# A depthwise wavelet convolution: from five tiles in two column phases to four in two and one in four

## The chip, the cores and the metric

The kernel runs on one core of a Trainium2 chip. The metric is the device time of one execution in microseconds; a kernel's time is the median of its runs. One further execution is taken by the hardware profiler, and all rows come from that one. TensorE (PE in rows; PEld is its weight load), VectorE (DVE), ScalarE (ACT), GpSimd (POOL) and SyncE (SP) each run their own instruction queue and synchronise by semaphores.

## What is computed

Two layers on an image batch `x` of shape (8, 96, 256, 256) in 32-bit floats. The first is a windowed linear attention and is not touched. The second adds to its input `x1`, after a group normalisation, a 5x5 depthwise convolution and a three-level Haar wavelet branch with its own 5x5 depthwise convolutions:

```python
for i in range(3):
    co = haar2d(cur)                 # four half-size images: sums and differences
    cur = co[:, :, 0]                # their low-pass one goes on to the next level
    flat = dwconv(co.reshape(B, C * 4, h, w), wconv_w[i]) * wscale[i]
    level_coeffs.append(flat.reshape(B, C, 4, h, w))
next_ll = zeros
for i in reversed(range(3)):
    next_ll = ihaar2d(level_coeffs[i] with next_ll added to its low-pass image)
out = x1 + dwconv(gn(x1), base_w) * base_scale + base_b + next_ll
```

The kernel folds level 1 of the wavelet and the base convolution into one linear map on the normalised image, so that only levels 2 and 3 are separate.

## The kernel before

The first stage computes the attention layer into `y_scratch` in device memory. The second stage, where the change lies, goes through the 96 channels, each in two groups of four images (192 groups). An image of 256 rows is cut into `WINDOWS = 5` tiles of 64 rows, of which 52 are kept (`OROWS`) and 4 on either side are halo. A tile stands on the partitions twice: 64 rows with the even columns and 64 rows with the odd ones (two column phases), 128 columns per image, 512 for four images. The convolution is then, per tile, five matrices of 128x128 (one per horizontal tap offset `d`), each applied to the tile shifted by `d`. Each 32-bit product is made as three matmuls of rounded parts: `split` issues high x high, high x low, low x high (L1312 to L1314). The results of the five tiles stay in five PSUM banks `ps_w`.

What each engine does for one group, in the order of its queue:

- SyncE (L1138 on): `group` waits until `make_x1` has freed the one pair of input buffers `xb`, `yb`, loads the rows of the group three ahead (10 DMAs), then `store` sends out the five output windows as they become ready. After the second group of a channel it loads the parameters and, once `mat23_ready` says that the last ones are used up, the raw matrices of the next channel with `load_raw` (10 DMAs).
- TensorE (`steps`, L1324): convolution of tiles 0 and 1; level 3 (20 matmuls, L1351 to L1354); level 2 (30 matmuls with 256 columns); tiles 2 to 4; the upsampling of `next_a` and `next_b` into all tiles (L1364, L1366); then `sum_down` (L1320) of the next group, which makes the low-pass image `ps_ll` for levels 2 and 3. `conv(t)` waits for `out_ready`, which says that VectorE has emptied the PSUM bank.
- VectorE (`steps`, L1465): `finish` of window 0 of the group before (bias and `x1` added, two column phases, L1458); `make_in`; `finish` of window 1; `split_in`; `finish` of windows 2 to 4; `make_x1` of the group two ahead (L1389); `trailing` of the next group, the low parts of its tiles (L1402, L1405); `up_levels`; `split_next`, which makes `next_lo`.
- ScalarE (`steps`, L1280): copies and high parts of levels 2 and 3; `norm` of the next group (16 operations, L1263); `leading`, its high parts (L1276 with a mask of zeros for rows beyond the image, L1278); the copy of level 3; the high parts of `next_ll` (L1297, L1298).
- GpSimd (L1216 on): `build` turns raw matrices into high and low parts: the convolution's once per channel, when `raw_in` says that they have landed (L1205, L1213), those of levels 2 and 3 when level 2 of the channel's second group is done (`l2_ready`).

At the start of the stage GpSimd sets whole buffers to zero (L1095) before SyncE issues the first raw load.

Of the kernel before, what the change touches and what calls it, by code (L numbers as in the profile page):

```python
# [21 lines left out]
F32 = mybir.dt.float32  # L22
F32R = mybir.dt.float32r
ALU = mybir.AluOpType
# [19 lines left out]
TAPS = 5  # L44
HALF = W // 2
WROWS = 64
# [9 lines left out]
NV1 = 4 * TAPS * 2  # L56
# [7 lines left out]
CHUNKS = PIECE // 512  # L64

# [8 lines left out]
def wt_attention_kernel(nc, x, wqkv_t, wp_t, gamma, beta, base_w, base_b, base_scale, wconv, wscale,  # L74
# [10 lines left out]
    with ExitStack() as ctx:  # L85
# [128 lines left out]
        with ExitStack() as ph:  # L214
# [62 lines left out]
            def _(pool):  # L277
# [30 lines left out]
                p1 = pad1.rearrange("p (ia q dj o n) -> p ia q dj o n", ia=2, q=2, dj=TAPS, o=2)  # L308
                for ia in range(2):
                    for q in range(2):  # L310
                        for oa in range(2):
                            for p in range(2):
                                o = 1 - p
                                first = WROWS - 3 - oa
                                full = p1[:, ia, q, :, o, first:first + 2 * TAPS - 1:2]
# [5 lines left out]
                                for n, dj in enumerate(djs):  # L321
                                    lo = first + 2 * dis[0]
                                    part = p1[:, ia, q, dj, o, lo:lo + 2 * len(dis) - 1:2]
# [692 lines left out]
        with ExitStack() as ph:  # L1016
# [14 lines left out]
            x1 = [sb_(f"x1_{s}", [128, PAIRW, IMGS, W]) for s in range(SLOTS)]  # L1031
# [3 lines left out]
            zb = [[sbr_(f"zb{g}_{h}", [128, WINDOWS, IMGS, ZW]) for h in range(2)] for g in range(SETS)]  # L1035
            raw1 = sb_("raw1", [128, 2 * TAPS, WROWS])
            raw2 = sb_("raw2", [128, 2 * TAPS, HALF])
            raw3 = sb_("raw3", [128, 2 * TAPS, HALF])
            mat1 = [[sbr_(f"mat1_{k}_{h}", [128, TAPS, 2 * WROWS]) for h in range(2)] for k in range(2)]
            mat2 = [sbr_(f"mat2_{h}", [128, 2, TAPS, HALF]) for h in range(2)]  # L1040
# [3 lines left out]
            down_sb = sbr_("down_sb", [128, WINDOWS, HALF])  # L1044
            UPPER = -(-(HALF // 2) // (OROWS // 2))
            LOWER = WINDOWS - HALF // OROWS
            up_sb = sbr_("up_sb", [128, UPPER + LOWER, 2 * WROWS])
            inside_sb = sb_("inside_sb", [128, PAIRW])
            mask = sb_("mask", [128, 2])
            zero1 = sb_("zero1", [128, 1])  # L1050
            z = sb_("z", [128, WINDOWS, IMGS, HALF])
# [21 lines left out]
            const_in, zeroed = sem_("constc_in"), sem_("zeroed")  # L1073
            xy_in, down_set, mask_set = sem_("xy_in"), sem_("down_set"), sem_("mask_set")
# [14 lines left out]
            NRAW = (4 + 2 + 4) * 16  # L1089
            GROUPS_C = C * SETS  # L1090

            def zero_pads(eng):

                for t_ in (xb, yb, *zb[0], *zb[1], *in2_p, in3_hl):
                    eng.memset(t_[:].bitcast(F32), 0.0).then_inc(zeroed, 1)  # L1095
                eng.memset(zero1[:], 0.0).then_inc(zeroed, 1)
# [6 lines left out]
            def slot(k, g):  # L1103
                return 2 * k + g
# [452 lines left out]
```

## Time and profile before

| | us |
|---|---|
| median of 3 runs | 10908.44 |
| lowest and highest run | 10892.28, 10910.33 |
| profiled execution | 10874.65 |
| its span | 10872.8 |
| second stage, from about | 5386 |
| TensorE busy over the span | 10462.5 (96%) |
| VectorE, ScalarE, GpSimd busy | 9149.1, 7181.6, 3711.4 |

The span is the time from the first instruction to the last; the profiled execution's own time is 1.85 us longer. Busy times are of one engine each and overlap between engines.

### The profile page before, as it was taken

To read this page: it belongs to the slowest core of one execution; us is meant where nothing else is said; L and a number is where in the kernel's file an instruction comes from. 1 tells how busy PE (TensorE), PEld (TensorE's weight loads), DVE (VectorE), ACT (ScalarE), POOL (GpSimd) and SP (SyncE) were. 2 spreads that over 40 slices of the span, in tenths; PEclk is the share of its full clock that TensorE was granted. 3 is DMA by queue.
4 is the path that set the end of the run, shared out by engine and by line. 5 is a ranking of instruction groups with operands and counts; after the bars stand their busy time and mean duration, and the time that the engine had idled before them with its cause. 6 is when DMAs were issued, how large, how long until landed. Compare 5 with 4: busy or idle time off the path is not lost.

```text
span 10872.8 us, 205183 instructions
## 1 busy us (share of the span) xinstructions
PE 10462.5 (96%) x66084; PEld 8922.4 (82%) x66084; DVE 9149.1 (84%) x16540; ACT 7181.6 (66%) x11852; POOL 3711.4 (34%) x3719
## 2 busy tenths in 40 slices
PE   4999999999999999999799999999999999999999
PEld 4888888888888888888678888888888888888887
DVE  6999999899999989988777777777777777777777
ACT  4887878778787777788555555555555555555554
POOL 3444444444444444444322222222222222222222
PEclk9999999999999999999899999999999999999999
DMA  5433333333433324322277777777777777777775
GB/s 188 136 95 127 113 113 132 106 119 102 136 113 109 130 92 136 112 72 81 71 155 153 157 157 154 155 153 154 158 155 155 154 153 155 158 154 156 154 152 125
DMA packets 1162869, 1453.49 MB, mean 134 GB/s; under 512 B 215391, under 2 KB 1125023, under 8 KB 1125279
## 3 DMA queue, kind: packets, MB, share of 16 engines
q1 hardware_dynamic: 1161055, 1442.80, 52.6%
q10 hardware_dynamic: 1376, 6.13, 0.1%
q8 instruction: 119, 1.95, 0.1%
q14 instruction: 319, 2.61, 0.1%
HBM read 1040.11 MB, written 408.56 MB: 133 GB/s over the span
## 4 chain that ended last, share of the span: by engine, by line
PE 28%; DVE 17%; issue 4%; ACT 1%; DMA 0%; SPq 0%; POOL 0%; DVEq 0%; POOLq 0%
PE ps_w L1312 5%; PE ps_w L1313 5%; PE ps_w L1314 5%; PE ps_ll L1320 4%; DVE ob L1458 4%; DVE x L1389 3%; DVE zb L1402 2%; DVE zb L1405 1%; PE ps_w L1364 1%; PE ps L1352 1%; PE ps_w L1366 1%; DVE sum L1429 1%; PE ps L1312 1%; PE ps L1313 1%; PE ps L1314 1%
## 5 line engine op out<-in xcount | busy, mean ns | idle before, releaser
L1312 PE MATMUL ps_w<-zb,mat 128*128 128x512 f32 x4800 | 1925.6, 401 | 8.8
L1313 PE MATMUL ps_w<-zb,mat 128*128 128x512 f32 x4800 | 1906.2, 397 | 0.0
L1314 PE MATMUL ps_w<-zb,mat 128*128 128x512 f32 x4800 | 1905.2, 397 | 0.0
L1458 DVE SCALAR_TENSOR_TENSOR ob<-ps_w,prm,x 64x512 f32<-64x512 f32 x1920 | 1440.7, 750 | 516.0 <-PE ps_w L1364 477.2
L641 POOL CAST xn_hi<-xs 96x512 fp32r<-96x512 f32 x1024 | 878.3, 858 | 2918.0 <-PE ps_qkv L666 2087.0
L1263 ACT ACTIVATE z<-x,prm 64x384 f32<-64x384 f32 (+1 forms) x3072 | 1813.7, 662 | 58.7 <-DVE x L1389 51.0
L1205 POOL CAST mat<-raw 128x1280 fp32r<-128x1280 f32 (+1 forms) x288 | 469.5, 1648 | 3942.6 <-DMA raw<-vec 2350.0
L664 PE MATMUL ps_qkv<-wqkv_hi,xn_hi 96*128 96x288 f32 x4096 | 1387.2, 339 | 47.1 <-issue 22.3
L643 POOL TENSOR_TENSOR xn_lo<-xs,xn_hi 96x512 fp32r<-96x512 f32 x1024 | 1355.8, 1324 | 81.9
L666 PE MATMUL ps_qkv<-wqkv_hi,xn_lo 96*128 96x288 f32 x4096 | 1212.1, 296 | 0.0
L665 PE MATMUL ps_qkv<-wqkv_lo,xn_hi 96*128 96x288 f32 x4096 | 1209.9, 295 | 0.0
L591 ACT ACTIVATE tok<-ps_qkv 128x1152 f32<-128x1152 f32 x1024 | 1160.4, 1133 | 0.0
L1312 PEld LDWEIGHTS ps_w<-zb,mat 128*128 128x128 f32 x4800 | 903.1, 188 | 303.1 <-DVE ob L1458 91.2
L1314 PEld LDWEIGHTS ps_w<-zb,mat 128*128 128x128 f32 x4800 | 901.9, 188 | 226.8
L1313 PEld LDWEIGHTS ps_w<-zb,mat 128*128 128x128 f32 x4800 | 901.6, 188 | 209.6
L686 PE MATMUL ps_num<-kv_sb,q_sb 104*128 104x104 f32 x8192 | 1070.2, 274 | 0.0
L702 PE MATMUL ps_f<-att,wp_sb 96*96 96x512 f32 x2048 | 1052.9, 595 | 8.2 <-DVE f_cur_b L176 3.1
L686 PEld LDWEIGHTS ps_num<-kv_sb,q_sb 104*128 104x128 f32 x8192 | 1026.4, 193 | 0.1
L1283 ACT ACTIVATE ll<-ps_ll 128x512 f32<-128x512 f32 x192 | 114.8, 598 | 1373.0 <-PE ps_ll L1320 1373.0
L559 ACT ACTIVATE att<-ps_t 96x512 f32<-96x512 f32 x1024 | 608.0, 594 | 602.5 <-PE ps_t L708 534.0
L791 DVE TENSOR_REDUCE ss<-sq 128x64 f32<-128x768 f32 x1024 | 965.6, 943 | 17.7 <-ACT sq L586 17.7
L1213 POOL TENSOR_TENSOR mat<-raw,mat 128x256 fp32r<-128x256 f32 (+1 forms) x1248 | 957.8, 801 | 34.7 <-POOL mat L1205 34.7
(202 smaller groups left out, 23976.0 us busy)
## 6 DMA issues: line engine op xcount, KB each, us to landing
xst<-in_x SPq DMA_DIRECT2D x96, 2048.0 KB, 14.1
xs<-in_x SPq DMA_DIRECT2D x128, 1536.0 KB, 9.0
y_scratch<-ys SPq DMA_DIRECT2D x128, 1536.0 KB, 9.6
out<-ob SPq DMA_DIRECT2D x768, 208.0 KB
xb<-in_x SPq DMA_DIRECT2D x576, 256.0 KB
yb<-y_scratch SPq DMA_DIRECT2D x576, 256.0 KB
raw<-vec SPq DMA_DIRECT2D x192, 320.0 KB, 4.3
raw<-vec SPq DMA_DIRECT2D x384, 160.0 KB, 4.0
```

The costliest lines, as they stand in the source:

```text
L591: s_.activation(tok[:, slot].rearrange("p g (t c) -> p g t c", t=3)[:, :, :, 0:C], ps_qkv[:, :, 0:3 * C].rearrange("p g (t c) -> p g t c", ...
L643: nc.gpsimd.tensor_tensor(lo, pixels(xs, k, j), hi.bitcast(F32), ALU.subtract).then_inc(xlo_ready, 1)
L664: mm(o, hi, wqkv_hi[:], start=True, stop=False)
L665: mm(o, hi, wqkv_lo[:], start=False, stop=False)
L666: last = mm(o, lo, wqkv_hi[:], start=False, stop=True)
L686: last = mm(ps_num[:, g, 0:QR], q_sb[:, slot, g * 128:(g + 1) * 128], kv_sb[:, g // 2, :], start=True, stop=True)
L702: mm(ps_y, wp_sb[:], att[:], start=True, stop=True).then_inc(y_ready, 1)
L1263: last = nc.scalar.activation(z[q * WROWS:(q + 1) * WROWS, ts, b, :], x1[slot(k, g)][rows, pairs, b, q::2], ACT.Identity, scale=prm[k][row ...
L1312: mm(out_, w[HI], xx[HI], start=start, stop=False)
L1313: mm(out_, w[HI], xx[LO], start=False, stop=False)
L1314: return mm(out_, w[LO], xx[HI], start=False, stop=stop)
L1458: last = v.scalar_tensor_tensor(out=ob[p:p + WROWS, t // 2].rearrange("p b w -> p (b w)")[:, q::2], in0=ps_w[t][q * WROWS:(q + 1) * WROWS, ...
```

## The change

The rows are cut differently: four tiles of 64 rows in two column phases and a fifth, "special" tile of 32 rows (rows 56 to 87, of which 60 to 83 are kept) in four column phases, 64 columns per image and phase, 256 for four images. Tiles at the image's edges start at the edge, so no mask is needed. The special tile needs three tap offsets instead of five, and its matrices are cut from the same padded vectors, which get two more offsets each. For it there are new buffers `x1_s`, `zq`, `zs`, `raw_s`, `mat_s`; ScalarE normalises it into `zn` and spreads it over four phases (`zq`). GpSimd adds its neighbouring columns (`sum_columns`: one sum, its high and its low part), from which `sum_down` takes the special tile's share. `sum_down` waits per tile. VectorE's order becomes: `finish` 0 and 1, `make_in`, `finish` 2, `split_in`, `finish` 3 and 4, `make_x1`, `up_levels`, `split_next`, `trailing`. ScalarE copies level 3 in the middle of `norm`, and `leading` comes last. SyncE issues the raw loads (18 DMAs) behind the loads of a channel's first group. GpSimd's order is written out per channel. At the start only the pads' edges are set to zero, and the summing matrices are built on the chip instead of loaded.

```diff
-NV1 = 4 * TAPS * 2
+NV1 = 4 * (TAPS + 2) * 2
...
+SROWS = WROWS // 2
+SPHASES = 128 // SROWS
+STAPS = 3
+BLOCKS = W // SPHASES
+SPECIAL = WINDOWS - 1
+TILES = ((0, 0, WROWS - HALO), (WROWS + SROWS - 4 * HALO, HALO, WROWS - 2 * HALO),
+         (H - 2 * WROWS + 2 * HALO, HALO, WROWS - 2 * HALO), (H - WROWS, HALO, WROWS - HALO),
+         (WROWS - 2 * HALO, HALO, SROWS - 2 * HALO))
...
+                    for ia in range(2):
+                        for q in range(SPHASES):
+                            first = q * SROWS + ia
+                            sp.dma_start(raw_s[first:first + SROWS - 1:2, :, :],
+                                         bass.AP(tensor=vec1.tensor,
...
                         if g == 0 and more:
                             load_gain(m * 2 + (k + 2), k)
+                    if g == 0 and (more or k == 0):
+                        sp.wait_ge(mat23_ready, m * 2 + (k + 1))
+                        load_raw(m * 2 + (k + 1))
                     store(m * 2 + k, g, m * 4 + (2 * k + g))
 
-                sp.wait_ge(zeroed, N_ZERO)
                 load_raw(0)
...
+                def sum_columns(qn, done, count, first=False):
+
+                    pool.wait_ge(done, count)
+                    pool.wait_ge(zn_set, qn + 1)
...
+                    nc.gpsimd.tensor_tensor(ls, rows_and_sums[SROWS:2 * SROWS, 0::2], rows_and_sums[SROWS:2 * SROWS, 1::2], ALU.add).then_inc(ls_set, 1)
...
+                def channel(c, k):
+                    sum_columns(c * 2 + 1, mat23_ready, c + 1)
+                    build_first(c + 1, 1 - k)
+                    sum_columns(c * 2 + 2, mat1_ready, c + 2)
+                    build_levels(c + 1)
...
+                    for b in range(IMGS):
+                        img = IMGS * g + b
+                        last = nc.scalar.activation(
+                            zn[:, b], x1_s[own(k, g), b], ACT.Identity,
...
+                    for q in range(SPHASES):
+                        last = nc.scalar.activation(zq[q * SROWS:(q + 1) * SROWS].rearrange("p b j -> p (b j)"),
+                                                    rows_and_sums[SROWS:2 * SROWS, q::SPHASES], ACT.Copy)
                     last.then_inc(z_set, 1)
...
+                        if t == SPECIAL:
+                            for d in range(STAPS):
+                                split(ps_w[t][:, 0:IMGS * BLOCKS], [mat_s[k][h][:, d, :] for h in range(2)],
+                                      [zs[g][h][:, :, d:d + BLOCKS] for h in range(2)], d == 0, False)
+                            return
...
+                        if t == SPECIAL:
+                            for v in range(2):
+                                last = mm(ps_w[t][:, 0:IMGS * BLOCKS], up_sb[:, UPPER_AT[t] + v, :], next_a[:, v::2],
+                                          start=False, stop=v == 1)
...
                     if before:
-                        finish(qn - 1, mb, kb, gb_, (0,))
+                        finish(qn - 1, mb, kb, gb_, (0, 1))
                     make_in(qn)
                     if before:
-                        finish(qn - 1, mb, kb, gb_, (1,))
+                        finish(qn - 1, mb, kb, gb_, (2,))
                     split_in(qn)
                     if before:
-                        finish(qn - 1, mb, kb, gb_, range(2, WINDOWS))
+                        finish(qn - 1, mb, kb, gb_, (3, 4))
                     if n is None or n + 2 < GROUPS_C:
                         make_x1(*ahead(m, k, g, 2))
+                    up_levels(qn)
+                    split_next(qn)
                     if n is None or n + 1 < GROUPS_C:
                         trailing(qn + 1, ahead(m, k, g, 1)[2])
-                    up_levels(qn)
-                    split_next(qn)
```

## Rows read from the trace of the kernel before

**Rows 1.** Windows view: window, length, busy PE, PEld, DVE, ACT, POOL, clock, DMA, GB/s.

```profile
5600.00:10860.00 5260.00, 5202.15 (x26345) 4300.56 (x26344) 4103.54 (x5971) 2928.49 (x5028) 1382.09 (x1484) 1.00 0.71 154
```

**Rows 2.** Chain of work in order of time: start, length, what; 191 groups apart.

```profile
5484.32 0.70 PE ps_w L1364 x3
...
10834.04 0.70 PE ps_w L1364 x3
```

**Rows 3.** Timeline of TensorE: start, length, instruction, out and in, count, idle before.

```profile
8001.61 0.28 PE L1352 MATMUL ps<-in_hl,mat 128*128 128x256 f32 x1
...
8007.62 0.40 PE L1312 MATMUL ps_w<-zb,mat 128*128 128x512 f32 x1
...
8018.19 0.86 PE L1364 MATMUL ps_w<-next_a,up_sb 128*128 128x512 f32 x3
...
8019.59 2.53 PE L1320 MATMUL ps_ll<-zb,down_sb 128*128 128x512 f32 x10
8021.96 0.39 PE L1312 MATMUL ps_w<-zb,mat 128*128 128x512 f32 x1
...
8046.39 0.96 PE L1364 MATMUL ps_w<-next_a,up_sb 128*128 128x512 f32 x3 [0.28 <-DVE next_b L1446]
```

**Rows 4.** Waits, 5600 to 10860: engine, line, releaser: us in total, times, longest.

```profile
PE ps_w L1364 <- DVE next_b L1446: 49.2, 93, 1.3
```

**Rows 5.** Groups by line and shape, same stretch: busy us, mean ns, idle before.

```profile
L1312 PE MATMUL ps<-in,mat 128*128 128x256 f32 x1870 | 534.3, 286 | 0.0
```

**Rows 6.** Timeline of VectorE over two groups.

```profile
8018.80 1.51 DVE L1458 SCALAR_TENSOR_TENSOR ob<-ps_w,prm,x 64x512 f32<-64x512 f32 x2 [4.20 <-PE ps_w L1364]
8022.79 0.76 DVE L1412 TENSOR_TENSOR in<-ll 128x256 f32<-128x256 f32 x2 [2.48 <-ACT ll L1283]
...
8031.26 3.66 DVE L1389 SCALAR_TENSOR_TENSOR x<-yb,gain,xb 128x1024 f32<-128x1024 f32 x3
...
8035.51 1.89 DVE L1405 TENSOR_TENSOR zb<-z,zb 128x512 fp32r<-128x512 f32 x3
...
8038.98 1.47 DVE L1429 TENSOR_TENSOR sum<-s 128x256 f32<-128x256 f32 x1
...
8042.08 0.42 DVE L1435 TENSOR_TENSOR low<-up,ps 128x256 f32<-128x256 f32 x1
...
8045.21 1.13 DVE L1446 TENSOR_TENSOR next_b<-next_ll,next_b 64x512 fp32r<-64x512 f32 x1
8047.02 1.51 DVE L1458 SCALAR_TENSOR_TENSOR ob<-ps_w,prm,x 64x512 f32<-64x512 f32 x2 [0.69 <-PE ps_w L1364]
```

**Rows 7.** Timeline of ScalarE: a 256-element cast, then `norm`.

```profile
8024.12 0.42 ACT L1287 ACTIVATE in_hl<-in 128x256 fp32r<-128x256 f32 x1
8024.44 9.48 ACT L1263 ACTIVATE z<-x,prm 64x384 f32<-64x384 f32 x16
```

**Rows 8.** Timeline of GpSimd over one channel.

```profile
8016.37 0.72 POOL L1205 CAST mat<-raw 128x640 fp32r<-128x640 f32 x1 [24.12 <-DMA raw<-vec]
8017.27 1.84 POOL L1213 TENSOR_TENSOR mat<-raw,mat 128x256 fp32r<-128x256 f32 x3 [0.18 <-POOL mat L1205]
8035.69 4.48 POOL L1205 CAST mat<-raw 128x1280 fp32r<-128x1280 f32 x2 [16.59 <-PE ps L1314]
8040.35 7.96 POOL L1213 TENSOR_TENSOR mat<-raw,mat 128x256 fp32r<-128x256 f32 x10 [0.18 <-POOL mat L1205]
```

**Rows 9.** Timelines of SyncE, VectorE and GpSimd in the first channel.

```profile
5452.51 0.32 SPq L1150 DMA_DIRECT2D xb<-in_x  x1
...
5467.67 3.67 DVE L1389 SCALAR_TENSOR_TENSOR x<-yb,gain,xb 128x1024 f32<-128x1024 f32 x3 [3.83 <-DMA yb<-y_scratch]
...
5475.67 1.50 POOL L1205 CAST mat<-raw 128x640 fp32r<-128x640 f32 x1 [49.69 <-DMA raw<-vec]
```

**Rows 10.** Timelines of GpSimd and SyncE at the start of the stage.

```profile
5386.47 2.66 POOL L1095 MEMSET xb<- 128x3072 f32 x1 [49.95 <-POOLq L902]
...
5403.43 2.73 SPq L1131 DMA_DIRECT2D raw<-vec  x4
```

More of the change, by code:

```diff
@@ L1039, in wt_attention_kernel @@
             mat1 = [[sbr_(f"mat1_{k}_{h}", [128, TAPS, 2 * WROWS]) for h in range(2)] for k in range(2)]
+            mat_s = [[sbr_(f"mat_s{k}_{h}", [128, STAPS, 128]) for h in range(2)] for k in range(2)]
             mat2 = [sbr_(f"mat2_{h}", [128, 2, TAPS, HALF]) for h in range(2)]
@@ new lines, in build_first @@
+                def build_first(c, k, first=False):
+                    pool.wait_ge(raw_in, c * NRAW + NRAW)
+                    if not first:
+                        pool.wait_ge(out_ready, c * (2 * WINDOWS) + (LEAD - 2 * WINDOWS))
+                    pool.sem_inc(pool_turn, 1)
+                    build([(mat1[k], raw1[:].rearrange("p (d o) m -> p d (o m)", o=2)[:, :, ::-1], "p d m -> p d m"),
+                           (mat_s[k], raw_s[:].rearrange("p (d o) m -> p d (o m)", o=SPHASES)[:, :, ::-1],
+                            "p d m -> p d m")],
+                          mat1_hi, mat1_ready, c + 1)
@@ L1231, in loop_groups @@
+                sum_columns(0, zeroed, N_ZERO, True)
+                build_first(0, 0, True)
+                build_levels(0)
+                with pool.Fori(0, C // 2 - 1) as m:
+                    for k in range(2):
+                        channel(m * 2 + k, k)
+                channel(C - 2, 0)
+                sum_columns(C * 2 - 1, mat23_ready, C)
             def loop_groups(eng, steps):
@@ L1456, in finish @@
                                 dve.wait_ge(prm_in[k], mc * 16 + 16)
-                        for q in range(2):
+                        for q in range(SPHASES if t == SPECIAL else 0):
+                            last = v.scalar_tensor_tensor(
+                                out=ob[0:SROWS, t // 2].rearrange("p b w -> p (b w)")[:, q::SPHASES],
+                                in0=ps_w[t][q * SROWS:(q + 1) * SROWS, 0:IMGS * BLOCKS], scalar=prm[k][own(k, g), 1:2],
+                                in1=x1_s[own(k, g)].rearrange("p b w -> p (b w)")[:, q::SPHASES],
+                                op0=ALU.add, op1=ALU.add)
+                        for q in range(0 if t == SPECIAL else 2):
                             last = v.scalar_tensor_tensor(
@@ new lines, in _ @@
+                for rows, at in ((0, UPPER_AT), (64, LOWER_AT)):
+                    for t in at:
+                        start, skip, n = TILES[t]
+                        width = tile_place(t)[2]
+                        src = ident_sb[rows:rows + 64, (start + skip) // 2:(start + skip + n) // 2]
+                        for q in range(128 // width):
+                            which = at[t] + (q // 2 if t == SPECIAL else 0)
+                            for to in (0, 64):
+                                o = up_sb[to:to + 64, which, q * width + skip:q * width + skip + n]
+                                v.tensor_scalar(o.rearrange("p (a r) -> p a r", r=2), src.unsqueeze(2).to_broadcast(
+                                    [64, n // 2, 2]), 0.5, None, ALU.mult).then_inc(down_set, 1)
@@ L1497, in _ @@
+                dve.wait_ge(down_set, N_SET)
                 dve.wait_ge(zeroed, N_ZERO)
```

225 lines of the change are left out of this document (123 added, 102 removed).

## The prediction, made before the changed kernel was run

> **What bounds the kernel now.** I read the engine shares of the second stage first: from 5600 us on TensorE is busy for 5202 of 5260 us at full granted clock, VectorE for 78%, ScalarE for 56%, GpSimd for 26% and the DMA engines for 71% [rows 1]. The change lies wholly in that stage, apart from some preparation. A group is four images of one channel; there are 192, at (10834.04 - 5484.32) / 191 = 28.01 us each (the first of a group's upsampling matmuls, at two places 191 groups apart in the chain of work) [rows 2]. Then I followed one group on TensorE in the timeline, from the upsampling matmuls at 8018.19 to those at 8046.39: 28.20 us [rows 3]. The waits say that once per channel TensorE idles 49.2 / 93 = 0.53 us for `next_b` of VectorE [rows 4]. So a group needs 27.67 us of matmuls: 1.40 for 6 upsampling, 2.37 for 10 in `sum_down`, 6.01 for 50 of levels 3 and 2, and the rest, 17.89, for 75 of the convolution, 0.2385 us each [rows 3]. Matmuls with 256 columns follow each other in 6.01 / 50 = 0.120 us. The duration in the grouped list (286 ns for these) overlaps with the next and is not the price [rows 5]. The stage is bound by TensorE, but VectorE's chain arrives with nothing to spare in every second group.
>
> **Part 1, matmuls.** Before, 5 tiles x 5 taps x 3 = 75 with 512 columns. After, 60 of these and 3 x 3 = 9 with 256 columns: 15 x 0.2385 - 9 x 0.120 = 3.58 - 1.08 = 2.50 us less per group. Upsampling goes from 6 wide ones to 5 wide and 2 half ones: no difference if a half one with a strided operand costs 0.12, 0.24 us more if it costs as much as a wide one; I take the first. `sum_down` keeps 10. The new waits of each `sum_down` tile cost between nothing and 0.05 us each, 0 to 0.25 us a group; I take 0, as `conv` waits per tile now and the whole shows no gaps. TensorE then needs 27.67 - 2.50 = 25.17 us, and 192 x 2.50 = 480 us go. The 0.53 us wait goes too if `next_lo` comes earlier: 96 x 0.53 = 51 us.
>
> **Part 2, does everything else fit into 25.17 us?** All times are from the start of the upsampling matmuls, P. `sum_down` ends at 3.77, convolutions 0 and 1 at 10.9, level 3 at 13.3, level 2 at 16.9.
> VectorE: two `finish` windows from 0.6 (1.51 each [rows 6]), input sums from 4.4 as now (8022.79 - 8018.19 = 4.6), to 5.8; window 2 to 7.3, `split_in` to 8.4, window 3 to 9.9. The special window has four operations 32x256 from PSUM: 0.42 is a PSUM operation of 256 elements, 0.75 one of 512 [rows 6]; I take 0.48, so it ends at 11.8. `make_x1` takes 3.6 [rows 6] and ends at 15.4, `up_levels` waits for level 2 and ends at 18.5.
> ScalarE: casts to 6.2, then `norm`. Its 16 operations take 9.48 now, half with 384 and half with 256 elements; all become 256, at some 0.54, 8.6 in sum. Four new `zn` at 0.54 and four `zq` at 0.31 (the spacing of the 256-element cast) to 0.54 add 3.4 to 4.3, I take 3.4 [rows 7]. With `copy_s3` in between waiting for level 3, it ends at 19.5. So the `next` casts, which waited for VectorE before, now wait for ScalarE: 20.8, and `next_lo` at about 21.7, 3.5 us ahead of P + 25.17. `leading` now follows, five casts of 0.5 to 0.6 (0.31 for 256 elements is under 0.62 for 512), to 23.5; edge tiles lose their mask. `trailing` comes after `split_next`: four at 0.6 (three take 1.89 with their overlap [rows 6]) and a small one, 2.8, to 24.5. TensorE wants its first tile at 26.6. Both chains fit where GpSimd is quiet: this is the first-to-second-group boundary of a channel.
>
> **Part 3, GpSimd at the other boundary.** The raw matrices are now issued behind the first group's loads, 18 DMAs in place of 10, and the channel's stores are queued behind them. SyncE issues one per 0.7 us. The nearest row is the first channel, where raws stand behind loads too: first load 5452.51, `x1` 15.2 us later, raws used 23.2 us after the first load [rows 9]. The loads are 288 rows instead of 304 (0.6 us less), the eight `raw_s` DMAs add 1.0 us by bytes (0.2 on 1.64 MB that took 8.0 us behind the loads), 3.2 by pieces (1536 on 3840), 5.6 at the issue rate. First load at P + 15.5, so raws are in at P + 39.1 to 43.7; I take 2.4 for `raw_s`, nearest to the pieces as DMA work and issuing overlap, and P + 40.5. Then `build_first`, now 0.72 + 1.84 [rows 8] and 1.8 for `mat_s`, 4.4; `sum_columns`, 3 operations of 512 elements with waits, 3.5 (2.2 to 4.5); `build_levels` 4.48 + 7.96 with waits, 12.6 [rows 8]; between 0 and 2.5 us for VectorE holding it up, 1 taken. Sum: P + 62.0. Level 3 of the next channel wants it at 2 x 25.17 + 10.9 = 61.2. In between it was covered by 9 us (GpSimd done at 8040.35 + 7.96 = 8048.3, level 3 at 8046.39 + 10.9 = 8057.3). An excess lengthens the period, which gives the chain more time, so the stall is about half the excess, 0.4 us.
> At the same boundary GpSimd works beside `trailing`. VectorE operations with two SBUF inputs then stretch: `sum` takes 1.47 for 256 elements and `next_b` 1.13 for 512, where three `trailing` of 512 took 1.89 together, while `finish` keeps 0.75 [rows 6, 8]. `finish` of window 0 stands behind `trailing` on VectorE's queue, and convolution 0 of the next group waits for it: it must start by P + 27.4. `trailing` from 21.7 alone ends at 24.5; with five such holds of 0.7 (nearly 1.2 beside a cast) at 28 to 29.5, or at 25.5 if only one bites. Between -2 and +2, I take 0.6 us of stall. Together 1.0 us per channel: 96 us.
> The Trainium skill, "SBUF — State Buffer", section "Who interferes with whom", says that a VectorE operation with two SBUF inputs and a GpSimd operation that reads SBUF exclude each other for a whole instruction. By it every one of the five would wait, which points to the upper end, 2 us per channel or 96 us more than my sum; the rows agree on who stretches.
>
> **Part 4, ends.** Zeroing held the first raw load from 5386.5 to 5403.4 [rows 10]; now only edges are zeroed and SyncE does not wait, but issues 8 more DMAs: about 12 us earlier. The longer `vec1` is behind the statistics of the first image. The last group ends as before within 0.5 us.
>
> **The sum.** 480 + 51 + 12 - 96 = 447 us less. The profiled run took 10874.65 (span 10872.8), giving 10428; the median of the three runs is 33.8 higher, so I forecast 10461.
>
> **Rivals.** (a) No stall at the boundary: 10461 - 96 = 10365. For it: three `trailing` operations ran in 1.89 us although a GpSimd cast was issued 0.18 us after the first [rows 6, 8]; it was the cast that waited. (b) The boundary costs 3.4 us per channel: both effects at their upper ends. 10461 + 2.4 x 96 = 10691. Against it: a late level 3 lets `trailing` and `finish` catch up, so they do not add fully. (c) Slower than before: the raw chain becomes the loop. The period before is 56.02, after 50.34 plus the stall; it is slower from a stall of 5.8 us on, an excess of 11.6, that is raws in at P + 52 rather than 40.5. With raws at P + 56 the stall is 7.7 and the time 10461 + 6.7 x 96 = 11104. The place is `build_levels` before level 3 of each first group. For it: `raw_s` comes in 1536 pieces of 128 bytes, and the raws share queue with 2.36 MB of loads. Against: DMA work per channel is 0.71 x 56 = 40 us, and even 5 us more leaves 50.3 us enough. The Trainium skill, "DMA: Bandwidth & Descriptors", section "Specifications", asks for 512 bytes or more for full rate, with read-modify-write below. Twice the price by pieces, 6.4 in place of 2.4 us, would move my sum by half of 4.0 us per channel, 190 us; the 256-byte pieces of `raw1` show no such step in a row of their own. (d) 256 columns of the special tile cost as much as 512 (the columns of each image are only 64 long): 9 x 0.1185 = 1.07 us a group back, 10461 + 205 = 10666; the level 2 matmuls, also 64 long, speak against it.
>
> **Chances.** Forecast 62%, (a) 12%, (b) 17%, (c) 6%, (d) 3%. The range 10360 to 10690 takes in (a), (d) and what lies between the forecast and (b); it leaves out about 15 to 20%. A measurement of this kernel tells 0.2%, some 22 us, from no change. Faster 92%, within 0.2% 2%, slower 6%, as only (c), and little of it, comes near no change.
>
> **What would show it.** Right: groups of 25.2 us from first to second of a channel and about 26.2 at the other boundary; 9 short matmuls at 0.12; TensorE above 96% in the stage; `next` casts directly after `zq`. Part 3 is wrong if TensorE waits for `mat` of level 3 (raws late) by over 1 us, or if the wait before convolution 0 is above 2 us. What would make the prediction wrong: raws landing 3 us or more later, `zn` and `zq` costing over 0.8 each (then `next_lo` binds both groups), or a load that `make_x1` waits for.

## The result and the profile after

The changed kernel takes 10842.63 us (median of 4, 10840.26 to 10849.04) against 10909.39 for the kernel before beside it: ratio 0.9943, 95% interval 0.9926 to 0.9960, 67 us less. The forecast was 447 less; 10842.63 is outside the range of 10360 to 10690, on the slow side. The profiled run took 10843.73 (span 10841.9), 416 us above the 10428 that the sum gives when it starts from the profiled run of before.

The distances between the upsampling matmuls of neighbouring groups tell where that went. They are worked out for all 192 groups from TensorE's timelines, and every run below is read by the same two numbers. "Behind first" is the distance from the upsampling of a channel's first group to that of its second (96 of them), "behind second" the one from there to the first group of the next channel (95). The upsampling of a second group is called the boundary between channels below.

| kernel | behind first, us | behind second, us | channel |
|---|---|---|---|
| before | 28.43 | 27.87 | 56.31 |
| after | 25.59 | 30.53 (29.04 to 31.79) | 56.11 |
| predicted | 25.17 | 26.2 | 51.3 |

The change saves 273 us behind the 96 first groups and loses 252 us behind the 95 second ones. With the start of the stage, 10 us earlier, that is the 31 us between the two profiled executions; the medians are 67 apart because the profiled execution of before lies 34 us under its median. One number ahead of the prediction was miscounted: the two rows of the chain [rows 2] lie 190 groups apart, not 191, so a group of before took 28.16 us, not 28.01. The sum was made of differences, so this moves no term of it. The predicted 25.17 has an error of its own: the group read in [rows 3] has a wait of 0.28 us in its row, and 0.53, the mean of all, was taken off it. Groups of before without a wait take 27.87, not 27.67.

The same stretch as [rows 1] in the windows view: TensorE is no longer always busy, and for the first time its clock is not 1.00.

```profile
5600.00:10780.00 5180.00, 4972.37 (x25107) 4082.53 (x25106) 4474.02 (x6273) 3547.45 (x6461) 2048.37 (x2316) 0.96 0.73 154
```

TensorE's timeline behind a second group, answering [rows 3]:

```profile
8022.08 0.64 PE L1453 MATMUL ps_w<-next_a,up_sb 128*128 128x512 f32 x2
8022.55 0.86 PE L1455 MATMUL ps_w<-next_b,up_sb 128*128 128x512 f32 x3
8023.25 0.62 PE L1450 MATMUL ps_w<-next_a,up_sb 128*128 128x256 f32 x2
8023.69 1.13 PE L1398 MATMUL ps_ll<-zb,down_sb 128*128 128x512 f32 x4
8025.35 0.74 PE L1398 MATMUL ps_ll<-zb,down_sb 128*128 128x512 f32 x2 [0.53 <-DVE zb L1491]
8027.01 0.74 PE L1398 MATMUL ps_ll<-zb,down_sb 128*128 128x512 f32 x2 [0.91 <-DVE zb L1491]
8027.68 0.73 PE L1402 MATMUL ps_ll<-ls,down_sb 32*128 32x512 f32 x2
8029.30 0.80 PE L1390 MATMUL ps_w<-zb,mat 128*128 128x512 f32 x1 [0.90 <-DVE ob L1550]
8029.90 0.63 PE L1391 MATMUL ps_w<-zb,mat 128*128 128x512 f32 x1
8030.32 0.63 PE L1392 MATMUL ps_w<-zb,mat 128*128 128x512 f32 x1
```

The ten matmuls of `sum_down` begin at 8023.69 and convolution 0 at 8029.30: 5.6 us for what took 2.37 before. From 8029.90 on the matmuls follow each other in 0.43 us, not 0.2385. The windows of one microsecond give the reason (busy PE is the second number, the clock the third from the end):

```profile
8026.00:8027.00 1.00, 0.09 (x1) 0.00 (x0) 1.00 (x2) 0.00 (x0) 0.82 (x2) 1.00 1.13 197
8027.00:8028.00 1.00, 0.99 (x3) 0.59 (x4) 1.00 (x2) 0.00 (x0) 1.00 (x2) 1.00 1.13 206
8028.00:8029.00 1.00, 0.41 (x2) 0.00 (x0) 0.98 (x2) 0.56 (x1) 1.00 (x2) 0.75 0.37 63
8029.00:8030.00 1.00, 0.70 (x2) 0.60 (x3) 0.97 (x2) 0.04 (x1) 1.00 (x3) 0.50 0.00 0
...
8034.00:8035.00 1.00, 1.00 (x3) 0.74 (x3) 0.98 (x2) 0.97 (x3) 0.38 (x1) 0.50 0.00 0
8035.00:8036.00 1.00, 1.00 (x5) 0.84 (x4) 1.00 (x3) 1.00 (x3) 0.00 (x0) 0.83 0.00 0
```

After the gaps the granted clock is 0.50 (1.2 GHz in place of 2.4) for some seven microseconds, most of them with TensorE fully busy again. It falls at 91 of the 95 boundaries, 451 us in all; in before it falls at none. Some 13 matmuls pay 0.19 us more each, 2.5 us. VectorE's timeline says who made the gaps, first behind the second group, then behind the first:

```profile
8018.79 0.69 DVE L1530 TENSOR_TENSOR next_a<-next_ll,next_a 64x512 fp32r<-64x512 f32 x1 [3.13 <-ACT next_a L1374]
8019.48 1.44 DVE L1532 TENSOR_TENSOR next_b<-next_ll,next_b 64x512 fp32r<-64x512 f32 x1
8020.95 6.00 DVE L1491 TENSOR_TENSOR zb<-z,zb 128x512 fp32r<-128x512 f32 x4
8026.87 0.95 DVE L1491 TENSOR_TENSOR zs<-zq,zs 128x256 fp32r<-128x256 f32 x1
8027.74 3.06 DVE L1550 SCALAR_TENSOR_TENSOR ob<-ps_w,prm,x 64x512 f32<-64x512 f32 x4
...
8051.40 2.50 DVE L1491 TENSOR_TENSOR zb<-z,zb 128x512 fp32r<-128x512 f32 x4
8053.82 0.42 DVE L1491 TENSOR_TENSOR zs<-zq,zs 128x256 fp32r<-128x256 f32 x1
```

`trailing` takes 6.00 + 0.95 us where GpSimd works and 2.50 + 0.42 where it doesn't (the four wide operations: 6.05 on average at the 95 boundaries), and `finish`, queued behind it, lets convolution 0 wait. GpSimd in the same stretch (compare [rows 8]):

```profile
8018.91 1.46 POOL L1256 TENSOR_TENSOR rows_and_sums<-rows_and_sums 32x512 f32<-32x512 f32 x1 [0.28 <-POOL mat_s L1246]
8020.53 0.85 POOL L1259 CAST ls<-rows_and_sums 32x512 fp32r<-32x512 f32 x1 [0.17 <-POOL rows_and_sums L1256]
8021.57 1.52 POOL L1262 TENSOR_TENSOR ls<-rows_and_sums,ls 32x512 fp32r<-32x512 f32 x1 [0.18 <-POOL ls L1259]
8023.04 3.37 POOL L1238 CAST mat<-raw 128x1280 fp32r<-128x1280 f32 x2
8026.59 7.79 POOL L1246 TENSOR_TENSOR mat<-raw,mat 128x256 fp32r<-128x256 f32 x10 [0.18 <-POOL mat L1238]
```

The boundary of before to compare with is the upsampling at 8046.39 [rows 3]; the one at 8018.19 belongs to a first group. GpSimd worked across that boundary too, but from 10.7 us ahead of it to only 1.9 us behind it, as the first matrices had been made a group earlier, beside 8018.19 [rows 8]; and VectorE had done `trailing` some 11 us ahead of it, before `up_levels`. Now `build_first`, `sum_columns` and `build_levels` follow each other without a gap, from 7.8 us ahead of the boundary (8014.33) to 12.3 us behind it (8034.38), and `trailing`, moved to the end of VectorE's order, begins 1.1 us ahead of it, in the middle of that work.

### The profile page after: what moved, and what is told of

Its sections match the earlier page's. It is cut to its first block, busy times and chain, and to the rows that moved or that the text cites. A ratio compares the mean times of both kernels' runs of the same rounds, so it can differ in the third digit from the quotient of the medians.

```text
span 10841.9 us, 210362 instructions
## 1 busy us (share of the span) xinstructions
PE 10286.2 (95%) x65124; PEld 8748.9 (81%) x65124; DVE 9571.3 (88%) x16952; ACT 7851.8 (72%) x13388; POOL 4393.2 (41%) x4595
## 4 chain that ended last, share of the span: by engine, by line
PE 39%; DVE 6%; ACT 3%; issue 2%; SPq 0%; DMA 0%; DVEq 0%
PE ps_w L1390 9%; PE ps_w L1391 8%; PE ps_w L1392 8%; DVE zb L1491 3%; PE ps L1438 3%; PE ps_ll L1398 2%; PE ps L1392 2%; PE ps L1390 2%; PE ps L1391 2%; ACT z L1336 1%; DVE ob L1550 1%; ACT zq L1342 1%; PE ps L1440 1%; DVE zs L1491 1%; PE ps_w L1455 1%
## 5 line engine op out<-in xcount | busy, mean ns | idle before, releaser
L1390 PE MATMUL ps_w<-zb,mat 128*128 128x512 f32 x3840 | 1629.2, 424 | 83.0 <-DVE ob L1550 83.0
L1336 ACT ACTIVATE z<-x,prm 64x256 f32<-64x256 f32 x3072 | 1641.6, 606 | 15.1
L1391 PE MATMUL ps_w<-zb,mat 128*128 128x512 f32 x3840 | 1597.1, 416 | 0.0
L1392 PE MATMUL ps_w<-zb,mat 128*128 128x512 f32 x3840 | 1594.1, 415 | 0.0
L1238 POOL CAST mat<-raw 128x1280 fp32r<-128x1280 f32 (+1 forms) x288 | 398.5, 1400 | 2855.2 <-DMA raw<-vec 2855.2
L1550 DVE SCALAR_TENSOR_TENSOR ob<-ps_w,prm,x 64x512 f32<-64x512 f32 x1536 | 1150.9, 749 | 34.9 <-PE ps_w L1453 5.1
L1390 PEld LDWEIGHTS ps_w<-zb,mat 128*128 128x128 f32 x3840 | 770.9, 201 | 339.2 <-DVE ob L1550 155.8
L723 PEld LDWEIGHTS ps_t<-ident_sb,att_t 128*96 128x96 f32 x4096 | 481.5, 125 | 586.2 <-issue 586.1
L1392 PEld LDWEIGHTS ps_w<-zb,mat 128*128 128x128 f32 x3840 | 768.4, 200 | 197.6
L709 PE MATMUL ps_g<-tok 128*104 128x97 f32 x8192 | 918.0, 255 | 0.0
```

The source lines that it names most:

```text
L1336: last = nc.scalar.activation(z[q * WROWS:(q + 1) * WROWS, ts, b, :], x1[slot(k, g)][rows, pairs, b, q::2], ACT.Identity, scale=prm[k][row ...
L1390: mm(out_, w[HI], xx[HI], start=start, stop=False)
L1391: mm(out_, w[HI], xx[LO], start=False, stop=False)
L1392: return mm(out_, w[LO], xx[HI], start=False, stop=stop)
L1550: last = v.scalar_tensor_tensor(out=ob[p:p + WROWS, t // 2].rearrange("p b w -> p (b w)")[:, q::2], in0=ps_w[t][q * WROWS:(q + 1) * WROWS, ...
```

## The experiments

Theory: `trailing` stretched by GpSimd, plus a fall of the clock behind the gaps, makes the 4.94 us by which the distance behind second groups exceeds the other. Rivals: mis-sized prices on VectorE and ScalarE (`zq` takes 0.67 us each, the special `finish` 0.69), or raw matrices that come too late. Each run below starts from the changed kernel. The first rival's rows, of ScalarE and VectorE in after:

```profile
8015.43 2.67 ACT L1342 ACTIVATE zq<-rows_and_sums 32x256 f32<-32x256 f32 x4
```

```profile
8037.85 2.75 DVE L1544 SCALAR_TENSOR_TENSOR ob<-ps_w,prm,x_s 32x256 f32<-32x256 f32 x4
```

**The clock alone.** Dummy matmuls in the gaps:

```diff
+                def warm(n):
+                    for _ in range(n):
+                        mm(ps_3[:].rearrange("p s n -> p (s n)"), down_sb[:, 0, :], next_a[:], start=True, stop=True)
...
+                        if keep:
+                            warm((0, 0, 3, 4)[t])
...
+                    if keep:
+                        warm(4)
```

> The kernel after, with eleven dummy matmuls of 512 columns (into the bank of level 3, already copied out) in each group that stands behind the second group of a channel: three before the wait of sum_down's third tile, four before the fourth's, four before convolution 0. TensorE would idle there anyway, about 3.5 us. Theory A, that the fall of the granted clock to 0.50 for 6 us behind this stall is a loss of its own: the clock stays at 1.00, about 13 matmuls take 0.24 instead of 0.43 us, 2.5 us per channel, 240 us: 10,605 us (10,570 to 10,680, as a dummy that ends late costs up to 0.3 us). Rival B, that VectorE and ScalarE set the period and TensorE's half speed falls into their slack: within 30 us of the kernel after, 10,840, or a little more.

Measured: 10680.29 us, 0.9813 of before (0.9796 to 0.9829); behind second groups 28.87 us, so 1.66 less. Eleven more matmuls made the kernel 1.3% faster. The clock is 1.00 throughout, while `trailing` is still long (5.5 us on average at the boundaries, 6.05 in after):

```profile
5600.00:10620.00 5020.00, 4986.00 (x26095) 4136.76 (x26094) 4431.03 (x6266) 3546.95 (x6457) 2055.62 (x2311) 1.00 0.76 159
```

So the fall is a loss of its own, 1.66 us per channel, not the 2.5 that I expected at the one place I had looked at: the distances of after alternate between about 30.0 and 31.3, and TensorE, now earlier, waits for GpSimd's matrices at 38 boundaries, 28 us in all:

```profile
8020.50 0.39 PE L1448 MATMUL ps<-in_hl,mat 128*128 128x256 f32 x1 [0.51 <-POOL mat L1246]
```

**GpSimd quiet.**

```diff
                     pool.sem_inc(pool_turn, 1)
+                    if c is not 0:
+                        pool.sem_inc(mat23_hi, 1)
+                        pool.sem_inc(mat23_ready, 1)
+                        return
```

> GpSimd doesn't build the matrices of levels 2 and 3 for any channel but the first (this leaves out that conversion, 12 us of GpSimd per channel; the raw matrices are still loaded, and the output of levels 2 and 3 of the other channels is made with the first channel's matrices). Theory A, that GpSimd's operations stretch trailing on VectorE from 2.5 to 6.0 us and so delay sum_down and finish at the boundary between channels: trailing back at about 2.5 to 3 us, no stall before convolution 0, no fall of the clock, both groups 25.5 us, 95 x 5.5 us less: 10,320 (10,280 to 10,400). Rival B, that the later next_lo of VectorE and ScalarE (zq and the special window cost more than I took) is enough to stall TensorE: 10,600 to 10,750. Rival C, that the raw matrices or another transfer hold the channel: 10,840.

Measured: 10394.01 us, 0.9552 (0.9536 to 0.9568); 25.59 and 25.84 us. 4.69 of the 4.94 us hang on the conversion of levels 2 and 3. `trailing` in the grouped list (busy us of all 768, then mean ns), first of after, then without the conversion:

```profile
L1491 DVE TENSOR_TENSOR zb<-z,zb 128x512 fp32r<-128x512 f32 x768 | 819.2, 1127 | 6.0
```

```profile
L1495 DVE TENSOR_TENSOR zb<-z,zb 128x512 fp32r<-128x512 f32 x768 | 590.0, 829 | 6.0
```

229 us of VectorE, 2.4 per channel, and no fall of the clock. Rival C is out: the raw matrices are still loaded, and those of the convolution are still used. This run alone doesn't separate the stretch from a late matrix. But in after TensorE never waits for a matrix in the stage, and the runs with GpSimd in another order, which keep all the work, settle it.

**The prices alone.**

```diff
-                                                    rows_and_sums[SROWS:2 * SROWS, q::SPHASES], ACT.Copy)
+                                                    rows_and_sums[SROWS:2 * SROWS, 256 * q:256 * (q + 1)], ACT.Copy)
...
-up_sb[:, UPPER_AT[t] + v, :], next_a[:, v::2],
+up_sb[:, UPPER_AT[t] + v, :], next_a[:, 256 * v:256 * (v + 1)],
```

(and `out` and `in1` of the special `finish` in the same way)

> Prices alone: zq and the special window's finish read and write 256 elements that lie side by side instead of every fourth, and the half-width upsampling matmuls read 256 columns side by side instead of every second. This changes what is computed in the special tile and nothing in the number of operations. If the step of the operands is what I mis-sized: zq 0.31 to 0.35 instead of 0.66 us each, the special finish 0.48 instead of 0.67, the half upsampling 0.12 instead of 0.22. If it is the 32 partitions or the offset between partitions: no change in these. The time itself: 1.3 + 0.8 us less per group on ScalarE and VectorE; if the stall at the boundary hangs on next_lo, 100 to 300 us less, otherwise the 0.2 us of the upsampling, 40 us.

Measured: 10656.76 us (one run; before 10881.98 beside it); 25.37 and 28.82 us. ScalarE, VectorE and TensorE in its timelines:

```profile
8033.40 1.70 ACT L1342 ACTIVATE zq<-rows_and_sums 32x256 f32<-32x256 f32 x4
```

```profile
8055.10 1.96 DVE L1544 SCALAR_TENSOR_TENSOR ob<-ps_w,prm,x_s 32x256 f32<-32x256 f32 x4
```

```profile
8015.83 0.40 PE L1450 MATMUL ps_w<-next_a,up_sb 128*128 128x256 f32 x2
8016.07 1.60 PE L1398 MATMUL ps_ll<-zb,down_sb 128*128 128x512 f32 x6
```

The step of the operands is the price: `zq` 0.42 instead of 0.67 us each (the 0.31 taken was too low even without a step), the special `finish` 0.49 instead of 0.69, a half upsampling 0.12 instead of 0.22. The last gives 0.21 us in every group; the first two bring `trailing` forward and give another 1.5 us behind second groups. Mis-sized prices thus feed the stall, but 3.4 us of it stay, and the clock still falls 69 times.

**GpSimd in another order**, the same work:

```diff
-                    build([(mat2, raw2[:, :, ::-1], "p s d m -> p (s d) m"),
-                           (mat3, raw3[:, :, ::-1], "p s d m -> p (s d) m")],
-                          mat23_hi, mat23_ready, c + 1)
+                    build([(mat3, raw3[:, :, ::-1], "p s d m -> p (s d) m")], mat3_hi, mat3_ready, c + 1)
+                    pool.wait_ge(z_lo, c * (2 * WINDOWS) + WINDOWS)
+                    pool.sem_inc(pool_turn, 1)
+                    build([(mat2, raw2[:, :, ::-1], "p s d m -> p (s d) m")], mat23_hi, mat23_ready, c + 1)
...
+                    sum_columns(c * 2 + 2, ls_lo, c * 2 + 2)
                     build_first(c + 1, 1 - k)
-                    sum_columns(c * 2 + 2, mat1_ready, c + 2)
```

> The kernel after, but GpSimd's work is put in another order: the column sums of a channel's second group before build_first of the next channel, then the matrices of level 3, and those of level 2 only once VectorE's trailing of the boundary is done; TensorE waits for level 3's and level 2's matrices separately. The same work, nothing left out. Theory A, that it is the overlap of GpSimd's conversions with trailing that costs 5.5 us per channel: trailing at 2.5 to 3.5 us, both groups 25.4 to 25.8 us, 10,350 to 10,450. Rival B, that the raw matrices' use is late anyway: the stall moves before level 3 or level 2, whose wait then shows, 10,600 to 10,850.

Measured: 10558.43 us, 0.9702 (0.9686 to 0.9718); 25.59 and 27.52 us. Better by 3.0 us per channel, but short of the forecast: level 3's conversion still lay beside `trailing` (VectorE, then GpSimd), and the clock still fell at 20 boundaries:

```profile
8048.11 5.05 DVE L1494 TENSOR_TENSOR zb<-z,zb 128x512 fp32r<-128x512 f32 x4
```

```profile
8049.38 5.24 POOL L1247 TENSOR_TENSOR mat<-raw,mat 128x256 fp32r<-128x256 f32 x5 [0.18 <-POOL mat L1239]
```

**One step further**: the wait on `z_lo` stands ahead of level 3 too.

> The kernel after with GpSimd's order of the last experiment but one step further: the matrices of level 3 as well as those of level 2 are only built once VectorE's trailing of the boundary between two channels is done (level 3 first, about 5.2 us, then level 2, 5.4 us). In that experiment level 3's conversion still ran beside trailing, which took 5.05 us. Theory A (GpSimd beside trailing is the cost): trailing 2.5 to 3 us, groups behind a channel's second group 25.6 to 26.2 us in place of 27.2, so 1.0 to 1.5 us per channel less: 0.956 to 0.960 of the kernel before. Rival B (the matrices of level 3, wanted about 11 us after the upsampling, or of level 2, 13.4 us after it, come too late instead): TensorE waits 1 to 3 us at level 3 or 2 and the time stays at 0.968 to 0.975 of before.

Measured: 10407.55 us, 0.9555 (0.9539 to 0.9571); 25.69 and 25.88 us. Theory A: `trailing` takes 3.45 us (somewhat over the 2.5 to 3 expected, as `build_first` still runs beside it), the matrices of levels 2 and 3 are begun behind it, none is late, and the clock never falls.

```profile
8071.55 3.45 DVE L1494 TENSOR_TENSOR zb<-z,zb 128x512 fp32r<-128x512 f32 x4
8074.92 0.41 DVE L1494 TENSOR_TENSOR zs<-zq,zs 128x256 fp32r<-128x256 f32 x1
```

```profile
8075.51 1.25 POOL L1239 CAST mat<-raw 128x1280 fp32r<-128x1280 f32 x1 [1.66 <-DVE zs L1494]
```

So 4.65 us behind second groups go with nothing but the order of one engine's work changed (and TensorE's wait split in two to match). **Without splitting the levels** the same gate is no cure. This run differs from the last in two more things: level 2 is built ahead of level 3, and the column sums stay behind `build_first`.

> The kernel after with one wait more: GpSimd builds the matrices of levels 2 and 3, in one piece as before, only after VectorE's trailing of the boundary between two channels. Theory A: trailing is beside build_first's end and sum_columns alone and takes 3 to 4 us in place of 6, so the stall before convolution 0 shrinks to under 1 us; but the matrices need 3.4 + 7.8 us and more from about 3 us after the upsampling on, are ready 15 us after it, and level 3 wants them 10.9 us after it: a new wait of 3.5 to 5 us at level 3, and a new fall of the clock there. The time is then within 1.5% of the kernel after, 10,700 to 10,950. Rival B: the gate alone is what the quick version needed, and splitting the two levels is not: 10,400 to 10,500.

Measured: 10752.15 us (one run; before 10868.60 beside it); 25.59 and 29.62 us. The wait moves to level 3, 1.94 us here and 2.15 on average where 3.5 to 5 were expected, and behind it the clock is 0.50 again:

```profile
8049.31 0.39 PE L1439 MATMUL ps<-in_hl,mat 128*128 128x256 f32 x1 [1.94 <-POOL mat L1246]
```

```profile
8050.00:8051.00 1.00, 1.00 (x6) 1.00 (x6) 0.97 (x3) 1.00 (x3) 0.83 (x2) 0.51 0.76 201
8051.00:8052.00 1.00, 1.00 (x6) 1.00 (x6) 0.97 (x2) 0.13 (x1) 0.82 (x2) 0.50 0.08 28
```

**The raw matrices back in their place**: `load_raw` after the channel's stores, ahead of the next first group's loads.

> One part of the change undone: the raw matrices are issued ahead of the loads of a channel's first group, as in the kernel before, not behind them. GpSimd waits 30 us per channel for them in the kernel after. Theory A: raws land 5 to 8 us earlier (2.36 MB of loads no longer stand ahead of them), but the matrices of levels 2 and 3 can't be built before level 2 of the channel's second group, about 17 us into that group, so GpSimd is still at work from 9 us before the boundary to 4 us behind it and trailing is still stretched: within 1.5 us per channel of the kernel after, 0.98 to 1.00 of before. Rival B: the placement behind the loads is what brings GpSimd's whole block onto the boundary; undone, only its last 3 us are left there and the stall shrinks to 1 us: 0.955 to 0.97. Rival C: the loads of x and y behind 18 more transfers come late, make_x1 waits for them: slower than before, 1.00 to 1.03.

Measured: 10984.06 us, 1.008 (1.0064 to 1.0097): slower than before, rival C. 29.84 and 27.71 us. `make_x1` of VectorE waits for the loads that now stand behind 18 transfers, which take SyncE 13.8 us to issue (8052.57 to 8066.38) where the 10 of before took 7.6; and the upsampling waits for `next_b`, TensorE's line below, 4.2 us on average at 93 boundaries:

```profile
8023.25 3.48 DVE L1479 SCALAR_TENSOR_TENSOR x<-yb,gain,xb 128x1024 f32<-128x1024 f32 x2 [4.47 <-DMA yb<-y_scratch]
```

```profile
8035.65 1.22 PE L1454 MATMUL ps_w<-next_a,up_sb 128*128 128x512 f32 x2 [4.22 <-DVE next_b L1533]
```

With 18 transfers and this shorter period the placement behind the loads is needed. But the 27.71 us say that it is also what brings GpSimd's work onto the boundary: undone, `trailing` takes 3.45 us there (at 8035.62), so theory A was wrong on that point and rival B had half of it.

**ScalarE's order**: `next` casts and wide `leading` casts ahead of `zq`.

```diff
-                    act.wait_ge(zn_set, m * 4 + (2 * k + g + 1))
-                    for q in range(SPHASES):
...
                     last.then_inc(z_set, 1)
...
+                    act.wait_ge(zn_set, qn + 1)
+                    for q in range(SPHASES):
...
+                    last.then_inc(zq_set, 1)
+                    act.wait_ge(zq_set, qn + 1)
                     nc.scalar.activation(zs[g][HI][:, :, 1:1 + BLOCKS], zq[:], ACT.Copy).then_inc(z_hi, 1)
```

> The kernel after with one change of ScalarE's order: the two next casts and the four wide leading casts come before the four zq copies instead of behind them (same work, nothing left out). This takes the mis-sized zq (2.67 us instead of 1.24) and its 1.2 us wait off the chain that leads to next_lo and trailing. Theory A, that the mis-sized prices of part 2 matter for the stall through this chain: trailing starts 2.5 us earlier at the boundary between channels, also if it still takes 5 to 6 us beside GpSimd; the waits of sum_down and most of that before convolution 0 (3.4 us with the thin stretch) go, and with them the fall of the clock: 3 to 5 us per channel, 0.955 to 0.970 of before. Rival B, that GpSimd's operations only bite more of the chain when it moves (they occupy the stretch from 7.7 us before the upsampling to 12 us after it): 0 to 1.5 us per channel, 0.98 to 0.994 of before.

Measured: 10659.33 us, 0.9781 (0.9765 to 0.9798); 25.72 and 28.61 us. Between the two: 1.9 us behind second groups. With GpSimd in its old place `trailing` still takes 6.12 us here and 5.0 on average, and TensorE, earlier where `trailing` is, now waits up to 2.8 us for the matrices of levels 2 and 3 at 54 boundaries.

```profile
8000.68 6.12 DVE L1494 TENSOR_TENSOR zb<-z,zb 128x512 fp32r<-128x512 f32 x4
```

**Both orders together.**

> Both cures together: GpSimd's order with the matrices of both levels behind trailing, and ScalarE's next and leading casts ahead of zq. Nothing left out. Theory A (the loss of the kernel after is wholly VectorE's chain at the boundary between channels, stretched by GpSimd and begun late behind ScalarE, and the fall of the clock that follows from it): both groups at 25.6 us, 51.2 per channel, granted clock 1.00, about 0.951 of before (0.949 to 0.956). Rival B (something else at the boundary, a late matrix or the stores, comes next): above 0.958.

Measured: 10466.55 us, 0.9603 (0.9587 to 0.9619): worse than GpSimd's order alone, with 26.50 us now behind first groups and 25.62 behind second. Behind a first group VectorE's small operation waits for the late `zq`, with `finish` queued behind it:

```profile
8036.87 0.42 DVE L1497 TENSOR_TENSOR zs<-zq,zs 128x256 fp32r<-128x256 f32 x1 [2.10 <-ACT zs L1355]
```

**`next` first, `leading` behind `zq`.**

> The kernel with all matrices of levels 2 and 3 behind trailing (10,408 us, 0.9555 of before), and on ScalarE the two next casts ahead of the four zq copies, with leading still behind zq. In the variant where leading came first too, VectorE's small trailing operation waited up to 2 us for the late zq and finish stood behind it. Theory A: next_lo comes 2.7 us earlier, trailing starts as before, so no new wait: both groups at 25.6, 0.953 to 0.9555 of before. Rival B: next_lo was not what cost the last 0.3 us of a channel; the same as without, 0.9555 +- 0.001, or 0.1 to 0.3 us per group worse as the casts now wait for VectorE's next_ll.

Measured: 10551.14 us, 0.9704 (0.9688 to 0.9720); 27.34 and 25.63 us: 1.65 us worse behind first groups than without. Rival B named the mechanism, ScalarE's casts waiting for VectorE's `next_ll`, but gave it 0.1 to 0.3 us. `zq` and `leading` are late by that wait:

```profile
8064.64 0.63 ACT L1376 ACTIVATE next_a<-next_ll 64x512 fp32r<-64x512 f32 x1 [1.89 <-DVE next_ll L1528]
```

```profile
8069.31 2.50 DVE L1494 TENSOR_TENSOR zb<-z,zb 128x512 fp32r<-128x512 f32 x4 [2.62 <-ACT zb L1351]
```

**Both orders, and the small operation of `trailing` behind `finish` 0 and 1** (GpSimd's gate opens after the four wide ones).

```diff
                         finish(qn - 1, mb, kb, gb_, (0, 1))
+                        trailing(qn, g, (SPECIAL,))
```

> As the variant with both cures (0.9603 of before), but VectorE takes the special tile's trailing operation out of the chain: it comes after finish of tiles 0 and 1. Theory A, that this one operation, waiting for the late zq with finish queued behind it, is why both cures together were slower than GpSimd's order alone: finish starts as soon as TensorE is through with the upsampling, no wait before convolution 0, both groups 25.6 us, 0.951 to 0.954 of before. Rival B (the matrices or make_in bind next): 0.956 to 0.961.

Measured: 10377.35 us, 0.9545 (0.9529 to 0.9560); 25.59 and 25.62 us, so by the two ratios 4.0% or some 434 us less than the change as made. TensorE has no gap left in the stage:

```profile
5600.00:10300.00 4700.00, 4700.00 (x24955) 3936.31 (x24955) 4314.64 (x6243) 3555.47 (x6423) 2112.79 (x2297) 1.00 0.80 169
```

Here `trailing` starts early enough that its stretch (4.03 us beside `build_first`) no longer reaches TensorE. This is the fastest version; the interval of its ratio overlaps that of 0.9555.

## Why the prediction was wrong

**Part 1 was right but for one term.** A group of before without a wait took 27.87, and with contiguous operands 25.37 is left: 2.50 us less, the sum's number, so 9 short matmuls at 0.12 hold and rival (d) is out. The strided half upsampling costs the other end of what I gave, 0.22: 0.21 us per group, 40 us in all. The waits of `sum_down` cost nothing where `trailing` is in time (25.59, no gap).

**Part 2, sizes.** `zn` 0.52 and `z` at 0.54 hold. `zq` is 0.67, not 0.31, the special `finish` 0.69, not 0.48. Behind first groups it all fits, as said; behind second ones it costs 1.5 us through `trailing`. The sum had no row for an operand that steps by four elements and took the spacing of a contiguous cast.

**Part 3 is where the prediction fell**: 1.0 us per channel was taken, 4.94 measured, 3.94 x 96 = 378 of the 416 us; upsampling makes 40. GpSimd's place was forecast well: `build_levels` from 1.9 us ahead of the boundary to 10.7 behind it, measured from 1.0 to 12.3 behind it. The 0.4 us for a late level 3 didn't come, as TensorE never waits for it. What failed is the other term, 0.6 us for `finish` standing behind `trailing`, in three steps.

First, the start of `trailing`. It was to start at P + 21.7 and, with five holds of 0.7 us, to end at P + 28.0. Behind the upsampling at P = 7996.49 it started at P + 24.5 (8020.95), 2.8 us late, and `finish` at P + 31.3 (8027.74). Of the 2.8 us, `zq` makes 1.4 (2.67 us where 1.24 were taken) and `next_b`, itself held by GpSimd, 0.75 (1.44 in place of 0.69); the rest I have not traced.

Second, the holds. They came to 4.0 us here, not 3.5. Rival (a), that they bite hardly at all, rested on three `trailing` operations in 1.89 us beside a cast [rows 6, 8]. The next row of that trace says otherwise. In before the `trailing` of an edge tile (L1402) stands once ahead of GpSimd's cast, with 0.74 us, and once beside it, with 1.74 us:

```profile
8034.84 0.74 DVE L1402 SCALAR_TENSOR_TENSOR zb<-z,mask,zb 128x512 fp32r<-128x512 f32 x1
...
8037.31 1.74 DVE L1402 SCALAR_TENSOR_TENSOR zb<-z,mask,zb 128x512 fp32r<-128x512 f32 x1
```

In after, beside GpSimd at work without a break, the four wide operations end at 8021.94, 8023.64, 8025.30 and 8026.95, each 0.54 to 0.55 us behind the end of a GpSimd instruction (8021.39, 8023.09, 8024.75, 8026.41): each waited for the GpSimd instruction under way to end. The Trainium skill ("SBUF — State Buffer", "Who interferes with whom") says so: a VectorE operation with two SBUF inputs contends with a GpSimd operation that reads SBUF, and the lock on the shared ports is exclusive. The trace agrees: 1.5 us for an operation that takes 0.62 alone, while `finish`, with one input from PSUM, keeps 0.76. I gave it as the upper end; it was the likelier reading.

Third, an idle TensorE was priced at its idle time alone. Behind the gaps the clock halves, 1.66 us per channel by the run with dummy matmuls, and no term, bound or rival had that. Without it 3.28 us are left, near the 3.4 of rival (b), which had the place but not the clock; but part of (b), a late level 3, was not there, so the nearness of the number is in part luck.

The three don't simply add up. Contiguous operands alone give back 1.5 us per channel, dummy matmuls alone 1.66, and GpSimd's order alone, which ends the holds of `build_levels` and with them the gaps, 4.65.

**The raw chain** had the forecast length, so rival (c) fell: 25.0 us from the first load (8044.69) to the use of the raws (8069.66), as from P + 15.5 to P + 40.5 in the sum, though both came 7 us later behind their upsampling. Its parts were not as forecast, so that the total fits is in part luck: SyncE issues without a gap from 8044.69 to 8066.46, the eight `raw_s` take 6.3 us of that and not 2.4, and the raws are in use 3.2 us behind the last issue. SyncE and GpSimd in after:

```profile
8044.69 0.68 SPq L1184 DMA_DIRECT2D xb<-in_x  x1
...
8055.52 6.28 SPq L1164 DMA_DIRECT2D raw_s<-vec  x8
...
8069.66 1.00 POOL L1238 CAST mat<-raw 128x640 fp32r<-128x640 f32 x1 [29.79 <-DMA raw<-vec]
```

The Trainium skill, "DMA: Bandwidth & Descriptors", "Specifications", asks for transfers of 512 bytes or more for full rate. The 6.4 us that I estimated by it for `raw_s`, in place of 2.4, are neither shown nor refuted, as SyncE's issuing fills 21.8 of the 25.0 us. **Part 4**: the first upsampling comes 10.4 us earlier (5473.75 against 5484.16), 12 were forecast.

So the forecast of 51.3 us per channel was reachable with a fitting order of GpSimd, ScalarE and VectorE (51.21, 10377 us), but not by the change as made.

## What to carry to other kernels

When a change shortens a loop, draw every engine's work against the new period, not only the chain that TensorE waits for: here GpSimd's work, which had ended 1.9 us behind the boundary, came to end 12.3 us behind it, and `trailing`, which had stood 11 us ahead of it, was moved into the middle of that work, where each of its operations waits for one of GpSimd's. Gate such work behind those operations and split it so that the part wanted first is built first. Price a gap of TensorE by what follows it too: look at the granted clock behind the longest gap of the trace. And an operand that steps over elements needs a row of its own.

## What the runs showed of the hardware

- Four VectorE subtractions of 128x512 float32, both inputs in SBUF, take 2.50 us alone and 6.00 beside GpSimd casts and subtractions that follow each other without a break. GpSimd is stretched too: a 32x512 subtraction takes 1.52 us instead of 1.28.
- Behind three gaps of 0.53, 0.91 and 0.90 us, all within 5 us, TensorE ran at a clock of 0.50 for 6.8 us, and behind a single wait of 1.94 us for 3.4 us, fully busy for most of it. Not every gap did it: in the run with level 3 still beside `trailing`, waits of 0.40 and 0.90 us before the same matmuls left it at 1.00 (it fell at 20 of 95 boundaries), and in the run with both orders together single waits of up to 1.1 us at 92 places never lowered it. What tells them apart stays open. Eleven dummy matmuls kept it at 1.00 and made the kernel 1.3% faster.
- 32x256 float32 with a step of 16 bytes: ScalarE 0.67 us in place of 0.42, VectorE (one input from PSUM, the other and the output with the step) 0.69 in place of 0.49. The Trainium skill, "SBUF — State Buffer", under "Door 1: The DMA port swizzle", says that an access crossing into a new line of 16 bytes pays; these two agree with that. By the same note a step of 8 bytes, two values to a line, should run at full rate, but a matmul's moving operand with it took 0.22 in place of 0.12 us; there the measurement decides.
